# A graph network on one core: semaphores cleared inside GpSimd's programs, and the first rows of three stages fetched ahead of the stage's border

## What is computed

```python
def attention(x):                       # origin, destination = src, dst
    x_norm = layernorm(x, ln_g, ln_b)
    q, k, v = (x_norm @ W + b for W, b in ((Wq, bq), (Wk, bk), (Wv, bv)))
    ws = einsum('ehd,ehd->eh', q[origin], k[destination]) * SCALE * edge_weights
    att = segment_softmax(ws, origin)
    values = segment_sum(att[:, :, None] * v[destination], origin)
    return x + (values @ W1 + b1) @ W2 + b2
def experts16(xf):                      # tw: two groups, two experts in each
    return sum(tw[:, e:e+1] * ((silu(xf @ W1[e]) * (xf @ W3[e])) @ W2[e]) for e in range(16))
def graph_conv(x, W0, W1, b):
    neigh = segment_sum(edge_vals[:, None] * (x @ W1)[edge_src], edge_dst, n)
    return relu(diag[:, None] * (x @ W0) + neigh + b)
def gnn(x):
    h = graph_conv(x, W0_1, W1_1, b1)
    return (graph_conv(h, W0_2, W1_2, b2) + x) * 0.5
def experts8(xf):                       # w: softmax of the two highest logits
    return sum(w[e] * layernorm(xf + relu(xf @ w1[e] + b1[e]) @ w2[e] + b2[e]) for e in range(8))
x = x + attention(ln(x)); x = x + experts16(ln(x)); x = x + gnn(ln(x)); return x + experts8(ln(x))
```

## Time and profile before

| | us |
|---|---|
| median of 3 runs | 2558.43 |
| lowest and highest | 2557.56, 2558.55 |
| the profiled execution | 2557.92 |
| its span | 2555.9 |

### The profile page before, as it was taken

How to read it: one execution, slowest core, us unless ns; L and a number is a source line. 1 busy time by engine, 2 the same in 40 slices (tenths; PEclk the granted TensorE clock), 3 DMA queues, 4 the chain that set the end, 5 groups by cost and what they waited for, 6 DMA issues and landing times. The chain is left out here.

```text
span 2555.9 us, 33503 instructions
## 1 busy us (share of the span) xinstructions
PE 2355.3 (92%) x10815; PEld 1862.5 (73%) x10818; DVE 1763.7 (69%) x4164; ACT 1135.7 (44%) x2077; POOL 692.0 (27%) x625
## 2 busy tenths in 40 slices
PE   6799895999999999999589999999977899999998
PEld 4577664777777777778467888888865677777776
DVE  7677796777877878786454765555555577777775
ACT  6554322444445454543342222222224756656652
POOL 5455012222222212210121312222222433333310
PEclk9899987999999999999799999999988899999999
DMA  5211032122121212210443344434346566666631
GB/s 164 50 51 50 18 128 92 64 85 93 57 99 54 95 59 90 81 64 33 133 161 101 123 148 131 132 128 132 127 138 192 109 163 154 142 163 155 145 100 50
DMA packets 156033, 271.89 MB, mean 106 GB/s; under 512 B 35442, under 2 KB 36082, under 8 KB 155638
## 3 DMA queue, kind: packets, MB, share of 16 engines
q1 hardware_dynamic: 122918, 203.00, 24.2%
q0 software_dynamic: 32976, 67.19, 11.6%
HBM read 185.82 MB, written 100.41 MB: 112 GB/s over the span
## 5 line engine op out<-in xcount | busy, mean ns | idle before, releaser
L2278 ACT ACTIVATE conv_h<-conv_h 128x512 f32<-128x512 f32 x79 | 49.9, 632 | 308.8 <-DVE conv_h L2230 308.8
L2723 POOL DMA_INDIRECT next_own<-message,net_slot_d x79 | 130.4, 1650 | 187.9 <-DMA next_own<-own 142.6
L2200 DVE TENSOR_TENSOR conv_yl<-conv_pty,conv_yh 128x512 fp32r<-128x512 f32 x79 | 54.7, 692 | 151.0 <-ACT conv_yh L2274 141.9
L1015 POOL DMA_INDIRECT early_val<-values,net_slot_s x79 | 86.1, 1089 | 190.0 <-DVE d_x L1467 88.8
L68 PE MATMUL d_po<-shared_wq_hi,d_hh 128*128 128x512 f32 x316 | 130.7, 413 | 7.1 <-DVE d_hl L1473 3.1
L1657 ACT ACTIVATE d_act_out<-d_pa 128x512 f32<-128x512 f32 (+1 forms) x80 | 46.2, 577 | 199.2 <-PE d_pa L70 199.2
L68 PE MATMUL conv_p<-conv_w_hi,conv_yh 128*128 128x512 f32 x316 | 132.5, 419 | 0.6 <-DVE conv_yl L2200 0.6
L68 PE MATMUL d_pc<-d_xh,shared_wv_hi 128*128 128x512 f32 (+1 forms) x320 | 129.3, 404 | 0.0
L68 PE MATMUL d_pa<-d_xh,shared_wk_hi 128*128 128x512 f32 (+1 forms) x320 | 129.1, 403 | 0.0
L68 PE MATMUL conv_p<-conv_w_hi,conv_hh 128*128 128x512 f32 x316 | 125.5, 397 | 2.1 <-DVE conv_hl L2200 2.1
L69 PE MATMUL d_pa<-d_xl,shared_wk_hi 128*128 128x512 f32 (+1 forms) x320 | 125.9, 393 | 0.0
(11 more groups left out here) (588 smaller groups left out, 7202.8 us busy)
## 6 DMA issues: line engine op xcount, KB each, us to landing
y<-d_y SPq DMA_DIRECT2D x79, 256.0 KB, 2.0
conv_yin<-y SPq DMA_DIRECT2D x79, 256.0 KB, 2.7
h<-conv_h SPq DMA_DIRECT2D x79, 256.0 KB, 2.0
own<-conv_own SPq DMA_DIRECT2D x79, 256.0 KB, 2.0
next_own<-own SPq DMA_DIRECT2D x79, 256.0 KB, 4.7
next_x<-y SPq DMA_DIRECT2D x79, 256.0 KB, 2.9
out<-d_res SPq DMA_DIRECT2D x79, 256.0 KB, 2.7
early_x<-in_x SPq DMA_DIRECT2D x10, 1024.0 KB, 6.9
```

Source lines behind the costliest of these rows:

```text
L1015: pool.indirect_dma_start(early.val[:, t, :], None, k.values[:, :], bass.IndirectOffsetOnAxis(ap=k.slot["s"][:, T * g + t:T * g + t + 1], ...
L2200: v.tensor_tensor(lo[:, t % 2, :], bank[t % 2][:], hi[:, t % 2, :].bitcast(F32), ALU.subtract)\
L2278: act_.activation(h[:, t, :], h[:, t, :], ACT.Relu).then_inc(h_made, 1)
L2723: pool.indirect_dma_start(own[n][:, t, :], None, k.message2[:, :], bass.IndirectOffsetOnAxis(ap=k.slot["d"][:, T * g + t:T * g + t + 1], a ...
```

## The change

`release` now only puts the semaphores aside; `Core.clear` clears what has been put aside and is called at four places inside POOL's programs (aggregation, dense0 after the last gathers, conv after the last fetch, and the program's end, there with one barrier). The second barrier at the borders is gone, and the Block's own barrier with its drains stays. `k.rows` becomes one buffer that outlives stages: it is the first buffer of `early`, then the rows of both message stages, and then holds the first message rows of the last stage. The weight `w11` is loaded and split at dense0's end, in place of `wk`. POOL issues the first 2 gathers of the first message stage at dense0's end, all 4 of the second at conv's end, and 4 plain gathers of the table `message` at the second message stage's end; the last stage's first group then has DVE add them instead of the accumulating gather. `y` rows for conv are loaded behind the store of tile 9. The order of conv's last group is written out anew, its own rows are waited for a stage later, and in dense0 and the projections DVE's order changes. The parts that the prediction speaks of, in the order of the file:

```diff
     def release(self):
-        if self.sems:
-            self.nc.clear_and_free_semaphores(self.sems)
-            self.nc.all_engine_barrier()
+        self.retired.extend(self.sems)
+
+    retired = []
+
+    @classmethod
+    def clear(cls, nc):
+
+        nc.clear_and_free_semaphores(cls.retired)
+        cls.retired.clear()
...
+        co = Core(nc, outer, "rows", side="right")
+        k.rows = co.sb("rows", [P, T, D])
+        k.rows_in = {n: [co.sem(f"rows_in{n}{t}") for t in range(T)] for n in (1, 2, 3)}
+        early = Early(Core(nc, keep, "early", side="right"), k.rows)
...
                 split_lo(v, g + 1, "s", 2)
+                split_lo(v, g + 1, "s", 3)
                 statistics2(v, g + 1, "d", s)
                 if g:
                     soft.part(v, g - 1, 3)
                 statistics3(v, g + 1, "d", s)
-                split_lo(v, g + 1, "s", 3)
...
             soft.part(v, EG - 1, part)
+        soft.low(v, EG - 1)
         w12_split(2)
         w12_split(3)
-        soft.low(v, EG - 1)
...
+        Core.clear(nc)
         power(0, early.rs[0], early.ve[0])
...
+def gather_sources(pool, k, stage, source, n):
+
+    pool.indirect_dma_start(k.rows[:, n % T, :], None, source[:, :],
+                            bass.IndirectOffsetOnAxis(ap=k.rec["d"][:, n, 0:1], axis=0),
+                            bounds_check=NROWS - 1, oob_is_err=False).then_inc(k.rows_in[stage][n % T], 16)
...
+                if c_ == NG - 2:
+                    sp.dma_start(w11_stage, chunks(a["g_w11"])).then_inc(w11_in, 16)
...
+                if g == NG - 4:
+                    Core.clear(nc)
...
-            power(NG - 1, 2)
+            for n, part in enumerate((slice(0, 2), slice(2, T))):
+                pool.wait_ge(stats[2], 2 * (NG - 1) + 2 * n + 1)
+                pool.tensor_tensor(rs[2][:, part], ve[2][:, part], k.half_neg[:, part], ALU.pow).then_inc(pow_done[2], 1)
+            for n in range(2):
+                pool.wait_ge(y_out[n], 16 + 16 * (NT // 2 - n))
+            for n in range(first_rows):
+                gather_sources(pool, k, 1, k.y, n)
...
+                first, second = slice(0, 2), slice(2, T)
+                back(g, u, 0)
+                w11_split(0)
+                back(g, u, 1)
+                v.wait_ge(squares_made, 4 * g)
+                v.wait_ge(stats[2], 2 * g)
+                mean(first)
+                v.wait_ge(y_made, 4 * g)
+                v.wait_ge(dev_made, g)
+                variance(first)
+                back(g, u, 2)
+                mean(second)
+                shift_dev(0, first)
+                variance(second)
+                shift_dev(1, second)
+                w11_split(1)
...
+                if g == 0:
+                    v.wait_ge(w2_high, 1)
+                    v.tensor_tensor(w["w2"][1][:], w2_stage, w["w2"][0][:].bitcast(F32), ALU.subtract).then_inc(w2_low, 1)
...
-            v.wait_ge(routed_in, 16)
-            v.wait_ge(consts, 2)
-            routing(0, {6: lambda: (add(1, 1, 0), add(1, 1, 1)), 10: lambda: (add(1, 1, 2), add(1, 1, 3))})
-            front1_begin(0, 1)
-            front1(0, 1)
+            for t in range(T):
+                add(1, 1, t)
             v.wait_ge(consts, 8)
             v.tensor_tensor(expert_r[:], expert[:], expert2[:], ALU.add).then_inc(expert_made, 1)
-            v.wait_ge(w2_high, 1)
-            v.tensor_tensor(w["w2"][1][:], w2_stage, w["w2"][0][:].bitcast(F32), ALU.subtract).then_inc(w2_low, 1)
+            front1_begin(0, 1)
+            v.wait_ge(routed_in, 16)
+            routing(0, {})
+            front1(0, 1)
...
+            act_.wait_ge(w11_in, 16)
+            act_.activation(w11[0][:], w11_stage, ACT.Copy).then_inc(w11_high, 1)
...
-            for n in range(ET):
-                t = n % T
+            for n in range(ahead, ET):
                 pool.wait_ge(turned, n + 1)
                 hold(pool)
-                pool.indirect_dma_start(rows[:, t, :], None, source[:, :],
-                                        bass.IndirectOffsetOnAxis(ap=k.rec["d"][:, n, 0:1], axis=0),
-                                        bounds_check=NROWS - 1, oob_is_err=False).then_inc(rows_in[t], 16)
+                gather_sources(pool, k, stage, source, n)
...
+            if empty_rows:
+                pool.wait_ge(zero_rows, 16)
+                for n in range(2):
+                    pool.wait_ge(stored[n], 16 + 16 * ET // 2)
+                pool.wait_ge(turned, ET + T)
+                for t in range(T):
+                    pool.indirect_dma_start(rows[:, t, :], None, table[:, :],
+                                            bass.IndirectOffsetOnAxis(ap=k.slot["d"][:, t:t + 1], axis=0),
+                                            bounds_check=EP + P - 1, oob_is_err=False).then_inc(k.rows_in[3][t], 16)
...
-            v.memset(sums[:], 0.0).then_inc(summed, 4)
+            v.memset(sums[:, T - 1, :], 0.0).then_inc(summed, 4)
...
-            for n, (source_, _, _, _) in enumerate(jobs[0:2]):
+            for n, (source_, _, _, _) in enumerate(jobs):
                 sp.dma_start(jobs[n][1][:], source_).then_inc(loaded[n], 16)
             beside.loads(sp)
-            if jobs:
-                sp.wait_ge(weight_low, 1)
-                beside.late_loads(sp)
             for g in range(EG):
                 for t in range(T):
                     sp.wait_ge(row_out, 4 * g + t + 3)
                     sp.dma_start(table[ds(g * GR + t * P, P), :], out[:, t % 2, :]).then_inc(stored[t % 2], 16)
                     beside.prefetch(sp, T * g + t)
                     if jobs and T * g + t == 9:
-                        sp.wait_ge(weight_low, 2)
-                        sp.dma_start(jobs[2][1][:], jobs[2][0]).then_inc(loaded[2], 16)
+                        sp.wait_ge(weight_low, 1)
+                        beside.late_loads(sp)
             for n in range(2):
                 sp.wait_ge(stored[n], 16 + 16 * ET // 2)
             if empty_rows:
                 sp.wait_ge(zero_rows, 16)
+                for n in range(2):
+                    sp.wait_ge(k.own_out[n], 16 + 32 * NG - 16 * n)
...
-            messages(nc, k, "msg1", k.y, w11, [(chunks(a["g_w11"]), yin, *w11), (chunks(a["g_w01"]), stage, *w["w01"]),
-                                               (chunks(a["g_w02"]), stage, *w["w02"])], k.message1, beside)
+            messages(nc, k, 1, 2, k.y, w11, [(chunks(a["g_w01"]), yin, *w["w01"]), (chunks(a["g_w02"]), stage, *w["w02"])],
+                     k.message1, beside)
...
-                store_own(g, T - 1)
+                if not last:
+                    store_own(g, T - 1)
...
-            group(NG - 2, LAST)
+            group(NG - 2, LAST, last=True)
             for t in range(LAST):
                 store_h(NG - 1, t)
+            store_own(NG - 2, T - 1)
             for t in range(LAST):
                 store_own(NG - 1, t)
-            for t in range(T):
-                sp.wait_ge(h_out[t], 16 + 16 * (NG if t < LAST else NG - 1))
-            for n in range(2):
-                sp.wait_ge(own_out[n], 16 + 32 * NG - 16 * n)
...
+            Core.clear(nc)
+            for t in range(T):
+                pool.wait_ge(h_out[t], 16 + 16 * (NG if t < LAST else NG - 1))
+            for n in range(T):
+                gather_sources(pool, k, 2, k.h, n)
...
+            g = NG - 1
+            turn_y(g, 1)
+            turn_h(g - 1, T - 1)
+            product_y(g, 0)
+            turn_y(g, 2)
+            product_y(g, 1)
+            turn_h(g, 0)
+            product_y(g, 2)
+            product_h(g - 1, T - 1)
+            turn_h(g, 1)
+            product_h(g, 0)
+            turn_h(g, 2)
+            product_h(g, 1)
+            product_h(g, 2)
...
-            gather(0, 0)
             gather(0, 1)
...
-            for n in range(2):
-                for t in range(T):
-                    scale_y(0, n, t)
+            for t in range(T):
+                scale_y(0, 0, t)
             half(0, 0, 0)
...
+            def add_message(t):
+                v.wait_ge(own_in[0][t], 16)
+                v.wait_ge(k.rows_in[3][t], 16)
+                v.tensor_tensor(own[0][:, t, :], own[0][:, t, :], k.rows[:, t, :], ALU.add).then_inc(first_added, 1)
+
             gains_of(0, 0)
+            add_message(0)
+            add_message(1)
             gains_of(0, 1)
...
+                if t + 2 < T:
+                    add_message(t + 2)
...
-            gains_of(0, 2)
             variance_of(0, 0)
             shifts(0, 0)
             for t in range(T):
                 low(0, 0, t)
+            gains_of(0, 2)
...
-            with ExitStack() as shared:
-                cs = Core(nc, shared, "shared")
-                hi, lo = ({n: cs.sb(f"{n}_{h}", [P, KC, D], F32R) for n in ("wq", "wk", "wv")} for h in ("hi", "lo"))
-                early = attention_phase(nc, a, k, shared, hi, lo)
-                dense0_phase(nc, a, k, hi, lo, early)
             with ExitStack() as between:
```

(10 more changed lines are left out.)

187 lines of the change are left out of this document (116 added, 71 removed).

## The result

| | before | changed |
|---|---|---|
| median (lowest to highest), us | 2558.43 (2557.56 to 2558.55) | 2525.51 (2520.82 to 2525.54) |
| profiled execution, its span | 2557.92, 2555.9 | 2520.82, 2519.1 |

The ratio is 0.9866 (95% interval 0.9844 to 0.9889): 33 us less, where 28 were forecast, inside the range. The same changed kernel was run in two of the later groups as well: 0.988 (0.9864 to 0.9897) with a median of 2525.83, and 0.9915 (0.990 to 0.993) with 2536.08. The gain is real each time, but a third of it comes and goes, and the experiments say in which stages.

What follows compares the result with a forecast made beforehand. TensorE was taken to be busy 92% of the span, with gains only where it stands, at stage borders and starts. The terms summed to -28.45 us, giving 2530 us as a median; the 8-in-10 range was 2515 to 2544.

Steps and rivals of the forecast that it cites:

- Second barriers: Borders between stages: thirteen second barriers go, at eight moments; those in no other term give -3.75 us.
- The clear in dense0: Within dense0, behind its last group's gathers: a drain of about 8 us fits in POOL's 12.56 us before the next power.
- Projections: Projection order: most of PE's 10.8 us of waits for `qkv_xl_s` go; -7.0 us (2 to 9.5).
- Dense0's start: Dense0's start: `expert_r` ahead of the routing and `w2_lo` later spare PE waits and low clock; -4.5 us (2.5 to 6.5).
- The sign that I had named: Dense0's start: PE busy above 6 of 10 us in the stretch after 445, where it was 4.86.
- Dense0's end: Dense0's end border: y stored 3.6 us earlier, but POOL's two gathers and 3.3 us drain come last; -0.7 us (-3 to +4).
- its rivals: Long drains: drains count all the stage's gathers, clear or not; dense0's 8.0 instead of 3.3 us, total 2538; chance 0.13.
- First messages: First message stage: SP's early loads set the third `msg_out` copy, 5.9 us earlier; less 0.7, -5.2 us (3 to 8).
- SP's loads are through sooner: First message stage rival: fewer transfers crowd the start, so the gain is up to 17 us, total 2518; chance 0.12.
- Conv's end and second messages: Conv's border no longer waits for the `own` store, -4.3 us; first scaling no longer waits for its gather, -5.1 us.
- Last stage: Last stage's start: four gathers and POOL's drain put the border at +9.2 us, first transpose at +22.5; +2.1 us (-3 to +4).

Runs made afterwards that it cites:

- later groups: Experiments ran in three groups: four kernels, then four on the same chip, then four on another chip; the changed kernel ran again in the first and third.
- The bare ones: Changed kernel with a further all-engine barrier, without a clear, behind each release: 13 at eight moments; median 2535.3 us.
- the experiment on the old start: Changed kernel with DVE's old order at dense0's start put back: 2539.31 us, 3.2 more than its base, the changed kernel rerun.
- the base of the first group: The changed kernel run again without any edit, as base of the first group of experiments: median 2525.83 us; the third group's base 2536.08 us.

## Why the prediction was right

The total was near, and mostly for its reasons. Point by point:

**Second barriers** (-3.75 for those in no other term, some 7.8 with all and their clears). The bare ones cost some 8 us by stages, so the term was of the right size. The clear in dense0 was expected to hide a drain of 8 us in the gap before the next power; it had nothing to hide, since its drain was over 0.1 us behind the last gather.

**Projections** (-7.0). In the first profiled executions it was -11.7 (257.1 to 245.4). Two sizes were off in that working: I took 7.6 of the 10.8 us of waits as gone for good and another 0.6 as lost at the tail, where all 10.8 went and 2.2 of them came back, which leaves 8.6; and I left out the clock, though a wait of PE is followed by matmuls at a lower one. PE's busy time in this stage, the sum rows of the windows from 64 to its end, before and after:

```profile
sum 257.00, PE 222.20 PEld 169.78 DVE 188.42 ACT 125.78 POOL 103.09; mean PE 37.03 PEld 28.30 DVE 31.40 ACT 20.96 POOL 17.18
```

```profile
sum 245.00, PE 218.79 PEld 167.31 DVE 188.32 ACT 125.48 POOL 102.53; mean PE 43.76 PEld 33.46 DVE 37.66 ACT 25.10 POOL 20.51
```

3.4 us less for the same matmuls. Against that, the stage of the changed kernel took 245 to 255 us from one group to the next, so the gain is anything from 2 to 12, and -7.0 fell into the middle by luck. I had no row that could have told of the late signals to ACT.

**Dense0's start** (-4.5). Undoing it costs 2.6 to 3.2: oversized, probably since I didn't carry `w2_lo` to its new place. In the first execution the term looked larger (PE's last product of dense0 5.5 us earlier behind the aggregation), and it hangs on the clock: in that execution and in the one before the change the full clock was back 12.4 and 12.3 us behind the stage's start, in the experiment on the old start and its base 19.8 and 19.9. The later return costs the new order 3.4 us and the old one some 0.8 (the second power of `early_sum_rs` in the kernel before and in that experiment). The sign that I had named, PE above 6 of 10 us in the stretch that was 445 to 455, is there in that execution alone: 8.9 us from 429.5 on, but 5.95 in the base of the first group and 5.9 in that of the third.

**Dense0's end** (-0.7). From PE's end to the border 14.1 us became 12.1, so -2.0. The steps hold: y stored 4.0 earlier where 3.6 were expected, POOL's drain last, 2.6 us behind the gather where 3.3 were expected. The drain is short only because of the clear; the working took for granted that the clear sets the count back, and put what it would cost otherwise among its rivals.

**First messages** (-5.2). Measured -4.6 from the border on. The step that decided it was not to count the 6 us of an earlier first product, since SP's loads set the third copy: 33.7 us behind the border, forecast 31 to 32. The store takes 4.4 us from issue to the copy instead of 3.5. The rival "SP's loads are through sooner" fell: the first store goes out 28.9 us behind SP's first load.

**Conv's end and second messages** (-4.3, -5.1). -3.2 and -6.5: the border a microsecond later than forecast, since POOL's four gathers and PE's last products end together, and the start a microsecond better.

**Last stage** (+2.1). +1.5 at the first transpose: the border came 9.4 us behind the last message store, forecast 9.2, and the transpose 12.6 behind the border, forecast 13.3.

**What is in no term, or in no experiment.** The aggregation got 3.0 us shorter, of which 1.2 are the second barrier ahead of it; the bare barriers gave 1.6 back. The early load and split of `w11`, the later loads of y and the new end of conv were not undone one by one, so what they gave is read from the traces alone.

## What to carry to other kernels

Issue a gather ahead of a border only where somebody else is later at that border than the gather's own drain: in conv this was worth 5 to 6 us, in dense0 and ahead of the last stage it cost 4 and 6, and the same gathers just behind the border were the better choice. Before counting what an earlier start is worth, look for a second queue that the stage meets a few tiles later; here SP's 28 us of early loads swallowed nearly all of it, and spreading them gave 10 us. And price a wait of PE by its length and by the matmuls behind it that run at a lower clock: in the projections 8.6 us of waits and 3.4 us of slower matmuls.

## What the runs showed of the hardware that was not expected

- A Block's drain on POOL takes about 0.08 us for each indirect DMA issued since the last drain or clear, even if all of them landed long ago. Behind POOL's last operation it ends 0.1 us with none, 0.4 with 4, 1.5 with 18, 1.7 with 20, 6.3 with 76, 7.8 with 95 and 8.0 with 97. Only the last stage's, most of them accumulating, cost less: 4.0 with 75.
- Gathers that were just issued set a floor instead: 2.6 us behind the last of two, 3.1 to 3.9 behind the last of 4 to 24. The two aren't added up: 97 with the last just issued took 8.0, and 79 at the end of conv before 6.5.
- A drain inside the clear ended 0.1 us behind its last gather in dense0 and in conv and yet set the count back.
- PE's signal to ACT can come up to 2.7 us behind the end that the profile gives its matmul, at the same place of the same code on one occasion and not on another. The projections of the changed kernel took 245.4 and 245.6 us without it and 254.9 with it, and 250.5 to 255.3 in the other kernels of the second and third group. Why was not found.
- After the low clock at dense0's start the full clock was back 12.4 us behind the stage's start in one execution of the changed kernel and 19.9 in the two others that were profiled, with PE busy alike; that moved the rest of the kernel by 3.4 us.
